# Layer 0's attention: scores and maxima per PSUM bank, exponentials per head from PSUM, new group order

## The reference, cut to what matters

```python
x = x + xattn0(layernorm(x), ctx, ctx, mask, ...)   # 16 heads of 8
x = x + ffn0(layernorm(x), ...)      # attention over the batch of 4, then experts (8, one per token)
x = x + xattn1(layernorm(x), ctx, ctx, ...)         # keeps the 32 largest scores
x = x + ffn1(layernorm(x), ...)                     # token shift, squared relu
```

```python
qm, km, vm = heads(q @ Wq.T + bq), heads(k @ Wk.T + bk), heads(v @ Wv.T + bv)
scores = einsum('bnlh,bnph->bnlp', qm, km) / sqrt(8)
scores = where(mask, scores, -1e8)
out = einsum('bnlp,bnph->bnlh', softmax(scores), vm)
return merge(out) @ Wo.T + bo
```

## Time and profile before

| | |
|---|---|
| median of three runs | 688.25 us |
| the profiled execution, first to last instruction (its span) | 689.4 us |
| busy in the whole span: TensorE, VectorE, ScalarE, GpSimd | 455.3, 512.7, 291.1, 263.1 us |
| the four groups of layer 0 | 40.2 to 260.4 us |
| the part before them (keys, values, loads) | 40.2 us |
| hand-over and the layer-1 tiles | 260.4 to 689.4 us |

### The profile page before, as it was taken

How to read it: one execution, slowest core, us unless ns; L and a number is a source line. 1 busy time by engine, 2 the same in 40 slices (tenths; PEclk the granted TensorE clock), 3 DMA queues, 4 the chain that set the end, 5 groups by cost and what they waited for, 6 DMA issues and landing times. The chain is left out here.

```text
span 689.4 us, 11334 instructions
## 1 busy us (share of the span) xinstructions
PE 455.3 (66%) x2460; PEld 338.7 (49%) x2460; DVE 512.7 (74%) x3078; ACT 291.1 (42%) x789; POOL 263.1 (38%) x404
## 2 busy tenths in 40 slices
PE   3759958747765777685678776775666748455445
PEld 2727744544652664353445554553455436444334
DVE  3644446966956963759989999979889799999800
ACT  3002222223222232443656677774656547553342
POOL 4010030032023022332556765655546646645442
PEclk9978977988897897766778888886887788665555
DMA  8030000000000000000000000000000000000000
GB/s 323 9 122 1 1 0 1 2 0 2 0 1 0 0 0 1 0 0 1 0 1 1 6 5 5 6 1 4 6 1 4 5 4 1 4 4 6 4 4 8
DMA packets 3816, 9.42 MB, mean 14 GB/s; under 512 B 808, under 2 KB 2992, under 8 KB 3376
## 3 DMA queue, kind: packets, MB, share of 16 engines
q1 hardware_dynamic: 3616, 7.96, 3.1%
q10 hardware_dynamic: 144, 0.88, 0.3%
HBM read 7.79 MB, written 1.05 MB: 13 GB/s over the span
## 5 line engine op out<-in xcount | busy, mean ns | idle before, releaser
L866 DVE MAX8 top<-area_b 128x8 f32<-128x77 f32 x768 | 112.1, 228 | 0.0
L877 DVE MATCH_REPLACE8 area_b<-top,area_b 128x77 f32<-128x77 f32 x512 | 106.9, 229 | 0.0
L374 POOL TENSOR_TENSOR e<-area_b 128x1232 f32<-128x1232 f32 x16 | 44.7, 2797 | 43.2 <-issue 23.0
L1168 PEld LDWEIGHTS psM<-vblk,pT 128*128 128x128 f32 (+1 forms) x320 | 54.3, 241 | 9.3 <-issue 9.3
L1154 PE MATMUL psT<-consts,e 128*128 128x128 f32 (+1 forms) x160 | 33.2, 331 | 38.6 <-POOL e L374 25.6
L1168 PE MATMUL psM<-vblk,pT 128*128 128x144 f32 (+3 forms) x320 | 53.7, 336 | 0.0
L877 DVE MATCH_REPLACE8 area_b<-top,area_a 128x77 f32<-128x77 f32 x256 | 53.5, 233 | 0.0
L998 PE MATMUL psM<-vblk,pT 128*128 128x144 f32 (+1 forms) x320 | 48.7, 314 | 6.8 <-DVE x L697 6.2
L362 POOL TENSOR_TENSOR d<-area_a,mxc 128x1232 f32<-128x1232 f32 x16 | 36.0, 2248 | 41.3 <-DVEq L893 41.3
L998 PEld LDWEIGHTS psM<-vblk,pT 128*128 128x128 f32 (+1 forms) x320 | 46.2, 214 | 8.8 <-ACT pT L445 5.3
L282 POOL TENSOR_TENSOR rstd_m<-veps_m,expo 128x4 f32<-128x4 f32 x8 | 8.4, 1050 | 109.9 <-DVE veps_m L648 109.9
(11 more groups left out here) (212 smaller groups left out, 1130.9 us busy)
## 6 DMA issues: line engine op xcount, KB each, us to landing
area_a<-in_w1T SPq DMA_DIRECT2D x1, 2048.0 KB, 14.7
area_b<-in_w SPq DMA_DIRECT2D x1, 2048.0 KB, 8.2
x<-in_x SPq DMA_DIRECT2D x1, 1024.0 KB, 9.4
out<-fin SPq DMA_DIRECT2D x16, 64.0 KB, 1.5
consts<-in_consts ACTq DMA_DIRECT2D x1, 862.0 KB, 5.0
weights<-in_weights SPq DMA_DIRECT2D x1, 836.0 KB, 6.5
rows<-in_rows SPq DMA_DIRECT2D x1, 576.0 KB, 11.3
ctx_sb<-in_ctxT SPq DMA_DIRECT2D x1, 154.0 KB, 4.7
```

The costliest lines, as they stand in the source:

```text
L374: e.tensor_tensor(p1.rearrange("p (h k) -> p h k", k=KEYS), ex1, cut, ALU.mult).then_inc(s["p_set"], 1)
L866: ins = e.max(top[:, r, h], (left if r else scores_sb[par])[:, h])
L877: ins = e.match_replace(left[:, h], top[:, r, h], (left if r else scores_sb[par])[:, h], GONE)
L1168: ins = mm(psM1[:, 0:VW], pT1[0:w, c], vblk1[0:w, t // NJ, c], start=(c == 0), stop=(c == NCH - 1), skip_group_check=True)
```

## The change

The scores of a tile are issued bank by bank: steps `s{b}0` to `s{b}3`, each with its mask matmul behind it and a signal of its own. VectorE takes the maxima of each bank by itself, negated (`mx{b}0` to `mx{b}3`). The subtraction is gone. ScalarE takes the exponential per head, 77 columns, from PSUM, with the negated maximum as bias (`e{b}0` to `e{b}3`, four heads each), and writes into `e0` or `d0` in turn. The factor 8^-0.5 moves from the exponential into the keys, and the mask's fill value is adapted. The scores of a bank wait for the exponentials of that bank of the tile before; `ta` waits for two banks of exponentials, `tb` and `tc` for all four. The group order is written anew: among others `b12` stands behind `v0`, `ta3` and `nm2` stand behind `ynorm`, and `v0` comes earlier against `among`'s steps.

```diff
-    rest = np.float32(MASK_FILL / SCALE)
+    rest = np.float32(MASK_FILL)
...
+        e0s = [e0[:], d0.rearrange("p h k -> p (h k)")]
...
-                    hold(e, s["s_made"], B * j)
+                    hold(e, s["s_made"], G * B * j)
...
-                    def exp():
-                        hold(e, s["s_sub"], u + 1)
-                        hold(e, s["t_turned"], 3 * u)
-                        e.activation(e0[:], d0.rearrange("p h k -> p (h k)"), ACT.Exp, scale=SCALE).then_inc(s["s_exp"], 1)
+                    def exp(g):
+                        def f():
+                            hold(e, s["s_max"], G * u + g + 1)
+                            if g == 0:
+                                hold(e, s["t_turned"], 3 * u - 3)
+                            for i in range(HG):
+                                h = HG * g + i
+                                ins = e.activation(e0s[b % 2][:, h * KEYS:(h + 1) * KEYS], scores_ps[:, g, i], ACT.Exp, bias=mx0[:, h:h + 1])
+                            ins.then_inc(s["s_exp"], 1)
+                        return f
...
-            e.tensor_tensor(k0[:], k0[:], mask_f[:], ALU.mult).then_inc(s["k0_masked"], 1)
+            e.scalar_tensor_tensor(k0[:], k0[:], SCALE, mask_f[:], ALU.mult, ALU.mult).then_inc(s["k0_masked"], 1)
...
-                    def highest():
-                        hold(e, s["s_made"], u + 1)
-                        hold(e, s["s_sub"], u)
-                        e.tensor_reduce(mx0.rearrange("p (g i) -> p g i", g=G), scores_ps, AX, ALU.max).then_inc(s["s_max"], 1)
-
-                    def subtract():
...
+                    def highest(g):
+                        def f():
+                            hold(e, s["s_made"], G * u + g + 1)
+                            e.tensor_reduce(mx0[:, HG * g:HG * g + HG], scores_ps[:, g], AX, ALU.max, negate=True).then_inc(s["s_max"], 1)
+                        return f
...
-                    def scores():
-                        hold(e, s["h_qT"], j + 1)
-                        hold(e, s["s_sub"], u)
-                        for g in range(G):
+                    def scores(g):
+                        def f():
+                            hold(e, s["h_qT"], j + 1)
+                            hold(e, s["s_exp"], G * u - G + g + 1)
                             mm(psS[:, g, 0:GW], q0T[32 * g:32 * g + 32, b], kblk0[32 * g:32 * g + 32, b].rearrange("p i k -> p (i k)"),
                                start=True, stop=False)
-                        for g in range(G):
-                            ins = mm(psS[:, g, 0:GW], mones[:], mrow[:, b].rearrange("p i k -> p (i k)"), start=False, stop=True)
-                        ins.then_inc(s["s_made"], 1)
+                            mm(psS[:, g, 0:GW], mones[:], mrow[:, b].rearrange("p i k -> p (i k)"), start=False, stop=True).then_inc(s["s_made"], 1)
+                        return f

                     def turn(g):
                         def f():
+                            hold(e, s["s_exp"], G * u + (G // 2 if g == 0 else G))
                             if g == 0:
-                                hold(e, s["s_exp"], u + 1)
                                 hold(e, s["t_copiedA"], 3 * u)
...
-                                ins = tr(psT[0:w, g % 2, (c % 4) * P:(c % 4 + 1) * P], e0[:, c * P:c * P + w], ident)
+                                ins = tr(psT[0:w, g % 2, (c % 4) * P:(c % 4 + 1) * P], e0s[b % 2][:, c * P:c * P + w], ident)
...
-GROUP_ORDER = """hstats zstats hrstd hnorm hturn hT zrstd znorm zturn hq zT q0 qs0 hqT s0 w12a mx0 sub0 q1 s1 w12b qs1 q2
-exp0 w12c0 mx1 ta0 qs2 q3 tb0 sub1 ca0 qs3 cb0 qk0 tc0 s2 b12 bias qk1 dot0 qk2 dot1 cc0 qk3 dot2 mx2 dot3
-v0 nm0 exp1 w12c1 ta1 ca1 soft tb1 cb1 ot0 mexp oT0 tc1 op0 softw x0 wv0 cc1 sub2 v1 wv1 zbias tot0 wv2
-tot1 exp2 s3 wv3 tot2 ta2 nm1 ot1 tot3 tb2 mturn ca2 oT1 mx3 op1 cb2 b12c xbias x1 tc2 sub3 mTc proj res
-cc2 v2 yrstd exp3 ta3 nm2 ynorm ca3 ot2 tb3 cb3 tc3 oT2 yaffine op2 x2 cc3 v3 ystore yturn yT nm3 ot3 lg
-oT3 gdiff op3 x3 gexp gate""".split()
+GROUP_ORDER = """hstats zstats hrstd hnorm hturn hT zrstd znorm zturn hq zT q0 qs0 hqT s00 s01 s02 s03 w12a mx00 mx01 e00 mx02 mx03  q1 e01 s10 e02  qs1 q2 mx10 s11 e03 w12c0 qs2 ta0 mx11 s12 q3 e10
+ca0 tb0 mx12 s13 w12b qs3 cb0 mx13 tc0  e11 cc0 qk0  bias qk1 dot0 e12 qk2 dot1 v0 e13 w12c1
+qk3 dot2 s20 ta1 nm0 ot0 dot3 mx20 s21 soft  oT0 mexp op0 softw e20 ca1 s22 mx21 tb1 x0 mx22 s23 b12 cb1 mx23 tc1 e21 cc1 wv0  wv1 tot0
+e22 v1 wv2 tot1 e23 b12c nm1 ot1 wv3 tot2 s30 ta2 mx30 oT1 s31 op1 tot3 mx31  e30 ca2 x1 s32 tb2 mturn mx32 s33 cb2 mx33 tc2 e31  cc2 mTc
+zbias xbias proj res yrstd e32 v2 e33  ynorm nm2 ot2 ta3 yaffine oT2 tb3 op2  ca3 cb3 tc3 x2 cc3 v3 ystore yturn yT nm3 ot3 lg oT3
+gdiff op3 x3 gexp gate""".split()
 
```

More of the change, by code:

```diff
@@ L213, in build @@
         mrow_made k0_masked kblk0_made kblk1_made ctx_rep v_turned v_masked den_cols xbo_made h_xn h_turned
-        h_xnT h_q h_qT s_made s_max s_sub s_exp t_turned t_copiedA t_copiedV pv_made pv_den pv_norm o_turned
+        h_xnT h_q h_qT s_made s_max s_exp t_turned t_copiedA t_copiedV pv_made pv_den pv_norm o_turned
         o_T o_proj x1_made q_z q_turned q_zT q_made q_stored zob_made m_prod m_sc m_sub m_exp m_w m_pv m_o
@@ L450, in turned @@
                         e.activation(at0T[:], psM0[:, 256:384], ACT.Identity, bias=Cl["bv"]).then_inc(s["o_T"], 1)
-                    return {f"exp{b}": exp, f"ca{b}": first, f"cc{b}": third, f"oT{b}": turned}
+                    return {**{f"e{b}{g}": exp(g) for g in range(G)}, f"ca{b}": first, f"cc{b}": third, f"oT{b}": turned}
                 steps = dict(hT=turned, hqT=queries)
@@ L697, in add @@
                         e.tensor_tensor(x1[:, t], psM0[:, 384:512], x1[:, t], ALU.add).then_inc(s["x1_made"], 1)
-                    return {f"mx{b}": highest, f"sub{b}": subtract, f"cb{b}": second, f"nm{b}": norm, f"x{b}": add}
+                    return {**{f"mx{b}{g}": highest(g) for g in range(G)}, f"cb{b}": second, f"nm{b}": norm, f"x{b}": add}
                 steps = dict(hstats=hstats, hnorm=hnorm)
@@ L1007, in project @@
                         mm(psM0[:, 384:512], at0T[:], Wt["wo0"], start=True, stop=True).then_inc(s["o_proj"], 1)
-                    return {f"s{b}": scores, f"ta{b}": turn(0), f"tb{b}": turn(1), f"tc{b}": turn(2), f"v{b}": value,
+                    return {**{f"s{b}{g}": scores(g) for g in range(G)}, f"ta{b}": turn(0), f"tb{b}": turn(1), f"tc{b}": turn(2), f"v{b}": value,
                             f"ot{b}": oturn, f"op{b}": project}
@@ L1083, in places @@
                     e.wait_ge(s["x1_made"], NT)
-                    e.wait_ge(s["s_sub"], NT)
+                    e.wait_ge(s["s_exp"], G * NT)
                     e.wait_ge(s["g_step"], 8 * (EARLY if early else NJ))
```

## The result

The changed kernel takes 748.75 us (median of five runs, 742.06 to 760.47), the kernel before on the same chip 688.58 (688.17 to 689.31). The ratio is 1.0857, 95% interval 1.0806 to 1.0908: some 60 us slower. (The ratio leaves out the run of 760.47 us, more than 1.5% above the fastest of its kernel, as a slow run.) The forecast was 20 us slower, 697 to 717 us, so its direction held and its size did not.

The account below looks back on a forecast made before the run. TensorE was taken to bind group 0, the order of steps groups 1 to 3; +9.2 us in group 0 and +11.1 in the others gave +20.3 on 688.25, so 708.5 us, range 697 to 717.

Parts of the forecast that it names:

- The maxima: VectorE, per bank of 308 columns: about 0.46 us each, taken as 0.40 back to back.
- the exponentials: ScalarE, 77 columns per head: 0.22 us a head, bounds 0.16 to 0.33; a tile 3.5 us instead of 1.2.
- VectorE's relief: VectorE without subtractions: about 1.1 us a tile net, nothing in group 0, 0 to 2.1 us gained per later group.
- The loss of the side-by-side passes: TensorE's scores bank by bank: nothing runs side by side, 2.05 us more a tile, 33 us of TensorE time.
- The clock: ... I count nothing: TensorE around v1 in groups 1 to 3: half clock costs little before; nothing added for the busier new order.
- the walk: New order followed through groups 1 to 3: qk0 at 10.1, v3 at 40.5 us; +3.7 a group, +11.1 together.
- Rival C: Behind v1, s30 to tc2 at half clock: 5.5 us of work, up to 4 us more a group, 720 us; chance 0.08.
- The bank alone, 0.83 us,: TensorE, one bank's two passes and mask: 0.83 us, from 0.66 (lower bound, passes 0.52) to 0.87.
- nm2's new place and ta3, 2.1 us a group: End of groups 1 to 3: nm2 behind ynorm, ta3 between ot2 and op2, delay v3 by 2.1 us.
- Group 0: TensorE's work on the path throughout: +9.2 us; +5.7 with the low bank cost, +10.5 with the high and exposed waits.
- Rival A: VectorE counts in groups 1 to 3: a bank under about 0.4 us, 13 us gained, 675 us; chance 0.07.
- B: Only group 0 pays; TensorE's gaps elsewhere absorb the banks, other groups within a microsecond; 697 us, chance 0.15.

Follow-up runs that it names:

- experiment 6: Kernel before with only the ScalarE part: one negated maximum a tile, no subtraction, sixteen exponentials from PSUM, two buffers; 694.64 us.
- experiments 1 to 4: Changed kernel with block of four banks again, 705.78 us; kernel before with masks between banks, 731.99; changed kernel without masks, 708.65; changed kernel with pairs of banks, 707.87.
- experiments 2 and 5: Kernel before with each mask right behind its bank, 731.99 us; kernel before with 18 extra mask matmuls ahead of each score block, 721.14 us.
- experiments 9 and 10: Changed kernel with ta3 and nm2 ahead of ynorm again, 732.79 us; changed kernel with 24 extra mask matmuls at each group's head, 751.44 us.
- experiment 8: Kernel before with only ta3 and nm2 moved behind ynorm; 698.46 us.
- experiment 7: Kernel before with only the new group order, block scores, one maximum and subtraction kept; 723.40 us.

## Why the prediction was wrong in size

**What held.** TensorE binds group 0, the order of steps the others. The maxima took what was priced, and so did the exponentials: sixteen in 3.72 us, 0.226 from start to start with the waits between banks and 0.21 without them (experiment 6), where 0.22 was forecast. VectorE's relief, 13 us in sum (forecast 16), shows nowhere as time gained. nm2 does stand behind ynorm, with ot2, ta3, tb3 and op2 between it and v3. The loss of the side-by-side passes, the term with most weight, is the first cause (experiments 1 to 4).

By the figures of the Trainium skill ("ScalarE: Activation LUTs", "What ACT_TABLE_LOAD costs") the prediction worked out 344 ns and a step of 251 for an exponential; this case measured 331 on average and a step of 0.21 to 0.22 us within a bank. The Trainium skill ("TensorEngine Tiling (Array Packing)", "Key Properties") states that a change of tiling mode drains TensorE. That agrees with the bank of 0.95 us, of which 0.52 would be the work of two passes by the prediction's lower bound; the trace shows the longer time, and not a drain as such.

**The step that failed first: "The clock: ... I count nothing".** Time at half clock went from 68 to 135 us. In group 2 the walk and the trace differ by 0.5 us at 191.6, when the fifth bank is done, and by 5.1 at qk0; between lies the first part of the half-clock stretch of 13.7 us. v1, in part at half, adds about 1.3 until proj, the way to v3 0.7, and v3 itself 2.5. Together, less 0.5 us that the head of the group was shorter, that is the whole 9 us by which this group missed its forecast (68.1 against 55.4 + 3.7). Rival C had the mechanism (a stretch at half clock) but the place and count wrong: it allowed 5.5 us behind v1; it is 13.7 us from q2 into v0, then v1, then v3.

What a us at half clock costs differs from place to place. The runs give 0.23 (experiments 2 and 5), 0.41 and 0.49 (experiments 9 and 10), and 0.30 between two profiles of the changed kernel's groups (275.1 and 285.4 us, with 134.6 and 169.3 at half). At 0.2 to 0.5 the 66 us more are 13 to 33 us of the 54.8 in the groups. Which of these is right for the whole kernel no run shows.

**The bank alone, 0.83 us,** was to lie between 0.66 and 0.87; it is 0.95 at full clock and 1.69 at half (47.75 to 49.43 us in group 0, where I had taken 1.66). The upper bound took the block's passes and one mask, and left out that the change back to the passes has a cost of its own, 0.1 us, paid per bank. 64 banks by 0.12 are up to 7.7 us of TensorE's time.

**nm2's new place and ta3, 2.1 us a group:** 3.2 in three groups (experiment 8), 3.3 us more in all. TensorE is idle for longer (3.62 us instead of 0.99 ahead of nm2's transpose), and transposes or v3 behind that run at half clock there.

**Group 0** was to lose 9.2 and lost 13.4 us. Its block at half clock is 6.6, as forecast. w12a behind it was to come wholly to the full clock and take 3.73 us; it takes 4.89, 1.2 more. The banks are 0.12 longer each at full clock, and the half-clock time is 24 instead of 14 us.

Added up for the profiled execution: the forecast for its span is 689.4 + 20.3 = 709.7 us; with at most 7.7 for the banks, 3.3 for nm2's place and 13 to 33 for the clock it is 734 to 754, where 740.3 was measured. The terms overlap (nm2's 1.1 a group is partly clock), and the price of the clock is loose, so this is a check of size and no ledger. Rival A is excluded by the bank's cost, B by 13 to 15 us lost in each loop group.

**What stays open:** why lone banks bring half-clock time when plain matmuls of the same sum don't, why the new order alone brings some too (experiment 7), and why groups with equal steps in one run get 31 or 51 us of it. The trace shows that it is so, not why.

## What to carry to other kernels

Here matmuls on 32 of TensorE's rows were cheap only while their neighbours in the queue were of the same shape (four banks in 0.73 us, one in 0.72): price a visit, not a matmul, and keep whatever interleaves (here the mask) behind the group. A finer hand-over between engines must gain more than the visits it adds; two banks at a time gave back nearly all. Where a forecast adds TensorE work in front of waits, give the half-clock time a term of its own, 0.2 to 0.5 us for each us that it may grow by these runs, or let the range reach that far. And before a change of clock is put down to an edit, look at a second profile of the same code: here equal code had 135 or 169 us at half.

## What the runs showed of the hardware beyond that

Two passes of a lone 32-row float32 bank take as long (0.72 us) as those of two banks (0.72) or four (0.73), and coming to a bank from another shape costs about 0.1 us more. A VectorE copy of 16 columns that normally takes 0.17 us took 2.75 when it started 0.09 us behind a GpSimd product of 1232 columns, and ended with it; as a maximum of two operands it fared no better (2.66 us at most), while MAX8 and MATCH_REPLACE8 on VectorE kept their 0.22 us beside GpSimd. One program varied by 18 us from run to run with the mean granted clock (731.32 us at 0.788, 749.85 at 0.770), and the changed kernel by 10 (742.06 us at 0.756, 751.83 at 0.739).
